# POOL's small fills ahead of all scatters, and the late experts' weights in two steps

## What is computed

```python
x = x + tanh(g_xattn) * xattn(layernorm(x), ctx, ctx)      # 16 heads of 16 values
x = x + tanh(g_ffn) * ffn(layernorm(x))
# ffn: swiglu(x @ sw1 + sb1) @ sw2 + sb2 for all rows (the shared expert)
#   + for each row its 2 likeliest of 8 experts, weighted by their softmax probability:
#     swiglu(x @ rw1[e] + rb1[e]) @ rw2[e] + rb2[e]
```

## Time and profile before

| | before |
|---|---|
| median of 3 runs | 738.01 us (737.25 to 738.84) |
| the profiled execution | 741.77 us |
| its span | 740.0 us |
| PE busy | 647.2 us (87%) |
| DVE busy | 501.3 us (68%) |
| ACT busy | 426.1 us (58%) |
| POOL busy | 242.4 us (33%) |
| mean granted PE clock | 0.943 |

### The profile page before, as it was taken

The page is one execution under the profiler, slowest core; times in us unless marked ns, Lnnn a source line. Parts: engine busy times, 40 slices in busy tenths (PEclk is TensorE's granted clock), DMA queues, the critical chain, the costliest instruction groups (busy, mean ns, idle before and its releaser), DMA issues.

```text
span 740.0 us, 12662 instructions
## 1 busy us (share of the span) xinstructions
PE 647.2 (87%) x3616; PEld 338.5 (46%) x3616; DVE 501.3 (68%) x829; ACT 426.1 (58%) x842; POOL 242.4 (33%) x240
## 2 busy tenths in 40 slices
PE   3788677879999999999999999978886969999990
PEld 3677451223233323333333332344364758888880
DVE  5799889748888888888888888547536734433430
ACT  3665244647777777777777777745523214544440
POOL 8342224033422443134000122100175503545542
PEclk9899897979999999999999999999987989999995
DMA  8879687925696687977566340010029994665545
GB/s 276 285 223 317 194 211 169 162 47 102 108 218 181 185 175 142 202 194 166 77 100 85 60 85 1 20 39 0 9 107 356 418 277 95 96 97 94 85 46 138
DMA packets 82858, 108.11 MB, mean 146 GB/s; under 512 B 16528, under 2 KB 64570, under 8 KB 81853
## 3 DMA queue, kind: packets, MB, share of 16 engines
q1 hardware_dynamic: 72080, 78.88, 45.7%
q0 software_dynamic: 10736, 28.71, 15.0%
HBM read 62.10 MB, written 47.35 MB: 148 GB/s over the span
## 4 chain that ended last, share of the span: by engine, by line
PE 66%; issue 14%; DVE 7%; POOL 5%; DMA 3%; another core or an unknown queue 2%; SPq 1%; POOLq 1%; ACT 0%; DVEq 0%; ACTq 0%
PE psO L1464 16%; PE psS L1437 16%; PE psM L1419 13%; PE psH L1682 7%; POOL parts L581 3%; PE psY L1708 3%; PE psX L1532 2%; PE psH L1638 1%; PE psH L1679 1%; PE psX L1670 1%; PE psH L1693 1%; DMA acc<-ysb,ids 1%; PE psO L1507 1%; PE psM L1437 1%
## 5 line engine op out<-in xcount | busy, mean ns | idle before, releaser
L810 ACT ACTIVATE pr<-psS 128x512 f32<-128x512 f32 x488 | 266.6, 595 | 109.2 <-PE psS L1437 109.0
L1073 DVE TENSOR_REDUCE mneg<-psM 128x1 f32<-128x1024 f32 x240 | 282.6, 1220 | 68.6 <-PE psM L1419 68.5
L1437 PE MATMUL psS<-qst,kst 99*128 99x512 bf16 x488 | 153.8, 388 | 12.1 <-DMA qst<-msb 11.5
L1464 PE MATMUL psO<-pr,vt 128*32 128x512 f32 x1024 | 138.3, 612 | 0.0
L1419 PE MATMUL psM<-kst,qst 96*128 96x512 bf16 x480 | 127.4, 386 | 6.4 <-DVE mneg L1073 4.1
L1437 PEld LDWEIGHTS psS<-qst,kst 99*128 99x128 bf16 x488 | 39.9, 97 | 160.5 <-ACT pr L810 129.9
L720 POOL DMA_INDIRECT acc<-ysb,ids x39 | 60.2, 1543 | 74.7 <-ACT ysb L933 43.9
L1419 PEld LDWEIGHTS psM<-kst,qst 96*128 96x128 bf16 x480 | 46.3, 98 | 65.5 <-DVE mneg L1073 10.6
L567 POOL TENSOR_TENSOR msb<-mcp,none 16x128 bf16<-16x128 f32 x16 | 6.2, 389 | 209.1 <-ACT mcp L787 209.0
L1682 PE MATMUL psH<-wall,zgT 128*128 x234 | 70.3, 437 | 0.0
L1308 DVE TENSOR_TENSOR rg<-psH,rs 128x256 f32<-128x256 f32 x39 | 16.6, 424 | 68.5 <-ACT rs L921 65.1
(11 more groups left out here) (244 smaller groups left out, 869.0 us busy)
## 6 DMA issues: line engine op xcount, KB each, us to landing
kst<-k_parts SPq DMA_DIRECT2D x96, 128.0 KB, 5.8
w_parts<-wraw POOLq DMA_DIRECT2D x14, 768.0 KB, 4.7
wall<-w_parts SPq DMA_DIRECT2D x7, 1536.0 KB
v_pad<-vst SPq DMA_DIRECT2D x16, 512.0 KB, 7.6
vt<-v_pad SPq DMA_DIRECT2D x16, 512.0 KB, 7.6
wraw<-wexp POOLq DMA_DIRECT2D x9, 768.0 KB, 6.7
k_parts<-parts SPq DMA_DIRECT2D x16, 384.0 KB, 6.1
qst<-q_parts SPq DMA_DIRECT2D x96, 64.0 KB, 5.3
```

Of the source, the lines that this page charges most:

```text
L810: nc.scalar.activation(pr[:, slot, j], score_bank(s, j), ACT.Exp, scale=SCALE).then_inc(e_done, 1)
L1073: V.tensor_reduce(mneg[:, parity, i:i + 1], psM[:, i % 2], X_AXIS, ALU.max, negate=True).then_inc(m_free, 1)
L1437: mm(score_bank(s, j), kst[:, slot, j, kt * P:(kt + 1) * P], qst[:, slot, j], start=True, stop=True).then_inc(s_full, 1)
L1464: last = mm(psO[j * VW:(j + 1) * VW, u % 2], vt[:, u, k, j * VW:(j + 1) * VW], pr[:, k % 4, j], start=(k == 0), stop=(k == KT - 1), skip_g ...
```

## The change

POOL works off its small fills before scatter(0) and then does all four scatters in one loop. SP issues the first late set's load (e = 0) after pv_done, b2_ok and wp_st, and waits for o_taken (the last attention tile is written) and at_full (it is turned) only ahead of e = 1.

```diff
--- before.py
+++ after.py
@@ -479,10 +479,12 @@
             sp.wait_ge(bp_st, 16 * 6)
             sp.wait_ge(b2_ok, 1)
             sp.dma_start(b2_sh[0:3], b2_parts[:, NR * D:NE * D]).then_inc(b2_in, 16)
-            sp.wait_ge(o_taken, UNITS + 1)
-            sp.wait_ge(at_full, NB)
             sp.wait_ge(wp_st, 32 * LATE)
             for e in range(LATE):
+                if e == 1:
+
+                    sp.wait_ge(o_taken, UNITS + 1)
+                    sp.wait_ge(at_full, NB)
                 sp.dma_start(wall[:, w_at(e):w_at(e) + WU].rearrange("p u c -> p (u c)").bitcast(F32),
                              w_parts[e]).then_inc(wl_ld, 16)
 
@@ -677,9 +679,6 @@
                             out_offset=bass.IndirectOffsetOnAxis(ap=slot_u[:, b, k * QT + t:k * QT + t + 1], axis=0),
                             in_=zx(b)[:, t], in_offset=None, bounds_check=SLOTS - 1).then_inc(sc_done if b < NB - 1 else sc_last, 16)
 
-            scatter(0)
-            scatter(1)
-
             pool.wait_ge(pv_done, 4 + KT * UNITS)
             pool.wait_ge(wp_st, 32 * LATE)
             nc.gpsimd.memset(fill, 0.0).then_inc(fill_c, 1)
@@ -696,8 +695,8 @@
             nc.gpsimd.iota(row_i[:, 64:], pattern=[[DRAIN, (TAB + 2) // DRAIN], [0, DRAIN]], base=0, channel_multiplier=0).then_inc(io_c, 1)
             pool.wait_ge(io_c, 8)
             nc.gpsimd.tensor_copy(rowc[:], row_i).then_inc(u_ok, 1)
-            scatter(2)
-            scatter(3)
+            for b in range(NB):
+                scatter(b)
 
             pool.wait_ge(h_full, 6)
             pool.wait_ge(sc_done, 16 * 2 * QT * (NB - 1))
```

## The result

| | before | after |
|---|---|---|
| median of 7 runs each | 738.84 us (737.25 to 742.29) | 746.09 us (742.64 to 746.89) |
| the profiled execution, its span | 741.77, 740.0 us | 746.89, 745.1 us |
| mean granted PE clock | 0.943 | 0.943 |

The ratio is 1.0077 (95% interval 1.0055 to 1.0100): slower by 5.7 us by the ratio and by 7.3 between the medians, where 7.8 us less were forecast, and outside the range of 722 to 742.

What follows compares the result with a forecast made beforehand. The prediction took SP's queue, backed up behind late weights, to delay the tile loop. An earlier tile start (5.0 us) plus a higher clock (2.8 us) gave 7.8 us off 738.01, so 730.2 us, range 722 to 742.

Steps and rivals of the forecast that it cites:

- (3): Start of the tile loop: tiles ready at 599.4, TensorE free at 599.8 and starting at 599.9, 5.0 us gained.
- the sum: Whole kernel: 5.0 us from the earlier tile start plus 2.8 us from the clock, 7.8 us gained.
- (1): POOL's fills ahead of scatter(0): 24 scatters end at 568.7, fourth batch and brow fills stay in place, no gain taken.
- What bounds the kernel: Ahead of the tile loop: late weights back up SP's queue, and TensorE sits idle for 5.07 us until the tile lands.
- The meeting of DVE and POOL: VectorE at 534 to 538 beside POOL's fills: might be held up to 0.8 us; nothing taken.
- (2): SP's late weights: first transfer issued at about 536, the other six from 540.6, SP free at 570.3.
- the feared new wait: Tile loop's start: TensorE waits there again behind a store or late batch; 733 to 736 us, chance 0.14.
- (4): TensorE's clock from 605 to 613: stays at 1.00 without the idle time, 2.8 us gained.
- Held answers: TensorE's products ahead of the tile loop: answers held back by one long scatter burst; slower, 744.3 us, chance 0.16.
- Until the burst's end plus 2.1 us: How long the slower case has TensorE's answers wait after POOL's 24 scatters: r_norm(3) until 570.8.
- Faster still: TensorE's answers ahead of the tile loop: lateness goes as the burst stands beside full queues; 722.6 us, chance 0.18.
- the two rivals: Outcomes for TensorE's answers: held longer by the burst, 744.3 us at 0.16, or lateness gone, 722.6 us at 0.18.

Runs made afterwards that it cites:

- g1: The changed kernel with POOL's wait counts as 16-bit numbers, same instructions otherwise: 725.28 us on chip 12 (ratio 0.9805), 744.66 us on chip 9 (1.0061).
- g2: The kernel before with POOL's wait counts as 16-bit numbers, same instructions otherwise: 741.71 us on chip 12, ratio 1.0008.
- g3: Against the kernel before, only the weights sent early, POOL's order kept, 16-bit wait counts: 728.80 us on chip 12, ratio 0.9852.
- k4: Against the kernel before, only the weights sent early, POOL's order kept, 16-bit wait counts: 730.18 us on chip 11, ratio 0.9865.
- k5: Against the kernel before, only the weights sent early, POOL's order kept, 16-bit wait counts: 726.88 us on chip 8, ratio 0.9826.

## Why the prediction was wrong, point by point

The step that failed is in (3) and in the sum: TensorE was taken to be free for the tiles at 599.8, as before, with no term for its own lateness. It was free at 612.31, because answers were held, and that outweighed the two terms that did come. Where nothing was held the same step failed the other way: in g1 TensorE was free at 586.6, the fourth batch's slots came at 567.2 where (1) had left them at 580, and the tile loads could leave earlier too. The gain was 10 to 15 us.

- **What bounds the kernel.** Right: SP's chain behind the late weights sets the tile loads, in every trace of the order before (602.01, 601.17, 602.81, 603.76). The margin was wrong. "TensorE sits idle for 5.07 us" was read as what the chain costs; it is 17.29 on a chip that holds nothing. The 5.07 came from a trace in which TensorE was itself late.
- **(1) POOL's fills.** 3.4 us from the memset to the first scatter (539.87 less 536.47), 3.3 forecast; 24 scatters at 1.295 us (569.66 less 539.87, over 23), 1.285 forecast. "That batch and the brow fills stay where they are" is false in both cases: the fourth batch moved by +10.9 us (590.96) with answers held, and to right behind the third without. The meeting of DVE and POOL, of which no row of before spoke, did occur, beside POOL's DMA of acc and not beside its copies: after has 0.52, 0.39 and 0.30 us for three short DVE operations from 537.94 on that took 0.24, 0.18 and 0.20 before, the first of them ending with that DMA's issue at 538.47. As they overlap, the next one starts only some 0.1 us later, so to take nothing was near enough.
- **(2) The weights.** Nearly right: after has the first issue at 537.89, 0.3 us behind that of b2_sh, the other six from 541.79 on, and SP free at 568.0 (forecast 570.3), with the last values copy 1.9 us later than in the trace that was forecast from.
- **(3) What is late next.** The tile loads, forecast near 596, left at 606.78 with answers held (brow fills done at 604.56 in place of 593.66) and at 588.53 without. With answers held the tiles were in time. Without, the feared new wait came, 4.29 us in g1, behind SP's table-row fills; the forecast had these out by 585 with nothing queued.
- **(4) The clock.** In size nearly right: 2.3 us against 2.8, clock 0.93 from 605 to 613. Both terms of the sum arrived, 5.07 and 2.3. What is missing from it is a third, TensorE's lateness: it is free 612.31 - 599.8 = 12.5 us later, 12.5 - 5.07 - 2.3 = 5.1. Of the 12.5, 1.9 us are there before the change acts (the last values copy is at 536.44, not 534.54).
- **The rivals.** "Held answers" with 744.3 is what came in the first comparison (746.1) and on chip 9 (744.7). That it came so near is in part luck, for its place was off by one answer: it had r_norm(3) wait until 570.8, but that came at 557.20, 20.8 us behind the values copy (22.1 before); first(0, 1)'s answer, next in line, was held instead, until 574.23. "Until the burst's end plus 2.1 us" was 3.6 after and 2.0 on chip 9 (574.06 less 572.08). "Faster still" with 722.6 is what came on chip 12 (725.3): r_norm(3) at 546.3 (549 there) and all scatters in one row, though its reason (full queues free the answers) isn't borne out, for on chip 12 the kernel before isn't held either, with hardly filled queues.
- **The chances.** 0.16 for held answers was too little. The rows of before showed held answers three times (a fourth, the first silu at 547.33 with 5.50 us idle, is in the trace but not in them), and one against. That row (565.94) lay beside the second, short burst. And the two rivals were weighed as two outcomes of one kernel anywhere, where the same kernel gave the one on chip 9 and the other on chip 12.
- **What the page on SBUF says.** The Trainium skill ("SBUF — State Buffer", "Who interferes with whom") says that TensorE and ScalarE never wait for another engine there. The rows don't contradict it: the 24 products of first(0, 1) and first(1, 0) have 5.86 us in after's record and 5.85 in those of g1 on either chip, and it is mainly what waits for them that starts late; what the gaps inside products are (1.8 us after) no row says. It was no argument against lateness by another route, as the prediction half took it to be.

**What is shown, and what isn't.** Shown: the slowdown is the held answers; the identical kernel has them on chip 9 and not on chip 12, with 744.7 and 725.3; the weights give the gain where nothing is held, and POOL's new order adds nothing to it that stands clear of the spread. Argued only: that it is a lasting property of a chip. Chip 12 showed none in any of its traces, before and after chip 9 did, chips 5, 8, 11 and 15 none; chip 9 was met once, with 8 runs that agree and one trace, and the chip of the first comparison is not on record. Open: the route by which an answer is held (the ends of products are modelled, but TensorE standing still in them can't explain what lies behind r_turn(3)'s start, 6.4 us after and 11.2 on chip 9, 574.06 less 562.82), and whether the unbroken burst or the full queues beside it stretch the holding. Against g2 (silu for first(0, 1) 14.3 us behind the values copy) that answer was 8 us late before (22.3) and 23.5 us late after (37.8). Weights only, with POOL's burst of 16 left as it was, is the version of choice where nothing is held, by its simplicity (726 to 730 against 725 to 730 for the whole change, within the spread), though in three of its five traces (g3, k4, k5) TensorE waits 5.4 to 5.7 us ahead of its first product with b2_sh, whose load now stands behind the weights. On a chip that holds it wasn't measured.

## What to carry to other kernels

Idle time ahead of a late transfer is not a measure of what the transfer costs until one knows that the waiting engine wasn't late itself: look for waits put down to "remote", and price the change with and without them. A change that takes away the bound of one chain makes the lateness of the other count: the medians of the kernel before lay between 738 and 742 us on every chip, those of the changed one at 725 to 730 or 745 to 746. And where a forecast rests on one trace, a second chip may tell more than a second run.

## What the runs showed that was not expected

- Answers of TensorE came some 22 us late beside a burst of indirect DMAs issued by POOL, on chip 9 and not on chip 12, for the same program. That the burst causes it is not shown. POOL's usual step is no sign, 1.29 us a scatter on both. But on chip 12 some scatters took longer (1.45 and 2.06 us, where 0.98 is usual), and on chip 9 none but the last of all (1.54). Where answers were held, the record had no landing of a scatter.
- TensorE's clock falls with the hole: from 560 to 580 it is 0.50 on chip 9 and 1.00 on chip 12, for the same program (busy 6.38 and 18.72 us). 0.50 is the lower level, 1.2 GHz.

```profile
560.00:580.00 20.00, 6.38 (x18) 5.04 (x19) 4.80 (x10) 2.86 (x5) 9.33 (x10) 0.50 1.01 409
```

```profile
560.00:580.00 20.00, 18.72 (x120) 15.78 (x121) 16.42 (x49) 7.06 (x11) 15.43 (x16) 1.00 1.02 396
```
